# Four-part kernel on sample pipeline: modulation rows behind the first packing, w1 split ahead of head 0, its bias row in two parts, identity turns in TensorE's waits, last sample's stage by halves

## What is computed

```python
# block 0: adapter with an expert per sample, then a layer norm
hidden = gelu(x @ down_W.T + down_b); hidden = expert_W[dom] @ hidden + expert_b[dom] + domain_emb[dom]
x = layernorm(hidden @ up_W.T + up_b + x) * ln_gamma + ln_beta
# block 1: modulated attention with 16 heads of 16 columns, and a feed-forward of 1024
emb = silu(sin_emb(timestep)) @ W_ada + b_ada; scale, shift = split(emb)
x = ln(x) * (1 + scale) + shift
probs = softmax(mask(q @ k.T / 4 + attention_bias)); x = x + (probs @ v) @ Wo + bo
h = ln(x) * g2 + beta2;  x = x + gelu2(h @ W1 + b1) @ W2 + b2
# block 2: one of three MLPs per sample, added to x, then a layer norm
# block 3: f = x; f_new = relu(f + dt * (-grad(A f) + 0.5 * grad2(B f))), differences along rows and columns
```

## Time and profile before

| | |
|---|---|
| median of 3 runs | 862.34 us (861.21 to 862.44) |
| profiled execution | 859.46 us, its span 857.7 us |
| busy | PE 94%, DVE 86%, ACT 73%, POOL 19% of the span |
| mean granted TensorE clock | 0.979 |
| slowest chain by engine | PE 85%, DVE 7%, SPq 2%, DMA 2%, issue 2%, ACT 1% |

### The profile page before, as it was taken

How to read it: one execution, slowest core, us unless ns; L and a number is a source line. 1 busy time by engine, 2 the same in 40 slices (tenths; PEclk the granted TensorE clock), 3 DMA queues, 4 the chain that set the end, 5 groups by cost and what they waited for, 6 DMA issues and landing times.

```text
span 857.7 us, 18597 instructions
## 1 busy us (share of the span) xinstructions
PE 808.4 (94%) x5968; PEld 692.9 (81%) x5968; DVE 737.6 (86%) x2473; ACT 622.8 (73%) x1285; POOL 164.1 (19%) x160
## 2 busy tenths in 40 slices
PE   5697899999999999999999999999999999999992
PEld 2585688988888888988888888888888888887782
DVE  6577777998989898998989898998989898979687
ACT  3447687878788797878788797878788787677541
POOL 3110112030211222040211222030211222111020
PEclk9779999999999999999999999999999999999997
DMA  4968877685867867575767767585658767484100
GB/s 131 267 170 213 196 172 187 138 174 155 183 157 190 169 158 196 140 180 146 187 149 188 177 158 198 126 189 152 177 155 182 179 152 185 117 177 126 57 25 25
DMA packets 147610, 137.33 MB, mean 160 GB/s; under 512 B 19299, under 2 KB 144804, under 8 KB 147509
## 3 DMA queue, kind: packets, MB, share of 16 engines
q1 hardware_dynamic: 145652, 134.99, 64.7%
q10 hardware_dynamic: 1856, 1.07, 0.7%
HBM read 98.23 MB, written 4.23 MB: 119 GB/s over the span
## 4 chain that ended last, share of the span: by engine, by line
PE 85%; DVE 7%; SPq 2%; DMA 2%; issue 2%; ACT 1%; POOL 0%; ACTq 0%; POOLq 0%; DVEq 0%
PE back_bank L1406 13%; PE turn_bank L1362 12%; PE score_bank L1606 7%; PE context_bank L1416 7%; PE score_bank L1607 6%; PE attend_bank L1400 5%; PE back_bank L1400 5%; PE front_bank L1400 5%; PE front_bank L1455 3%; PE back_bank L1386 3%; PE back_bank L1377 3%; PE attend_bank L1386 3%; PE front_bank L1719 3%; PE attend_bank L1347 2%; PE front_bank L1446 2%
## 5 line engine op out<-in xcount | busy, mean ns | idle before, releaser
L581 ACT ACTIVATE sc<-sc,negmax 128x256 f32<-128x256 f32 x512 | 231.4, 504 | 15.4 <-DVE negmax L1236 14.0
L1236 DVE CUSTOM_DVE_ANT_0 sc<-score_bank,side 128x256 f32<-128x256 f32 x512 | 195.3, 419 | 36.7 <-PE score_bank L1607 32.3
L575 ACT ACTIVATE pt<-turn_bank 128x512 f32<-128x512 f32 x176 | 106.1, 604 | 132.0 <-PE turn_bank L1362 111.0
L1362 PE MATMUL turn_bank<-ident,sc 128*128 128x128 f32 x1024 | 156.6, 276 | 1.8 <-ACT sc L581 1.7
L1362 PEld LDWEIGHTS turn_bank<-ident,sc 128*128 128x128 f32 x1024 | 123.3, 141 | 32.3 <-issue 14.1
L1606 PE MATMUL score_bank<-ks,qs 128*128 128x256 f32 x512 | 122.9, 322 | 5.8 <-DMA qs<-ql 5.4
L1406 PE MATMUL back_bank<-w,ffT 128*128 128x256 f32 x512 | 118.5, 379 | 0.4 <-DVE ffT L1145 0.4
L1406 PEld LDWEIGHTS back_bank<-w,ffT 128*128 128x128 f32 x512 | 96.7, 190 | 13.5 <-DVE ffT L1145 1.0
L497 POOL TENSOR_TENSOR rstd<-var,half_neg 128x2 f32<-128x2 f32 x64 | 49.9, 780 | 282.5 <-DVE var L998 281.0
L1607 PE MATMUL score_bank<-mask_neg,ident_r 128*128 128x512 f32 x256 | 102.4, 400 | 0.0
L1606 PEld LDWEIGHTS score_bank<-ks,qs 128*128 128x128 f32 x512 | 78.7, 193 | 13.8 <-issue 10.6
(11 more groups left out here) (272 smaller groups left out, 1966.3 us busy)
## 6 DMA issues: line engine op xcount, KB each, us to landing
side<-in_side SPq DMA_DIRECT2D x128, 512.0 KB, 5.4
qs<-qh SPq DMA_DIRECT2D x128, 64.0 KB, 4.2
qs<-ql SPq DMA_DIRECT2D x128, 64.0 KB, 4.4
ks<-kh SPq DMA_DIRECT2D x120, 64.0 KB, 4.0
ks<-kl SPq DMA_DIRECT2D x120, 64.0 KB, 4.4
wb<-in_wb SPq DMA_DIRECT2D x15, 512.0 KB, 7.2
xN<-in_x SPq DMA_DIRECT2D x16, 256.0 KB, 4.7
wc<-in_wc SPq DMA_DIRECT2D x16, 256.0 KB, 2.8
```

The costliest lines, as they stand in the source:

```text
L575: e.activation(pt[:, h % NP2, :, :], two(tbank[h % 2]), ACT.Copy).then_inc(copied[h % 4], 1)
L581: i = e.activation(sc[:, h % NS, q, :], sc[:, h % NS, q, :], ACT.Exp, bias=negmax[:, q, h:h + 1], scale=-1.0)
L1236: i = e.tensor_tensor_reduce(sc[:, s % NS, q, :], two(sbank[s % 2])[:, q, :], side[:, (H * X.i + s) % NSIDE, q, :], -1.0, 3.4e38, ALU.add, ...
L1362: i = e.transpose(tbank[h % 2][:, k * S + q * P:k * S + q * P + P], sc[:, h % NS, q, k * P:k * P + P], ident[:, :])
```

## The change

- SP: w1 is loaded right behind the column pack, and the mask and side pair 0 stand ahead of sample 1's x. All five grids are loaded ahead of the store of the modulation rows. `load_ada` of sample 1 moves from slot 5 to slot 8 of turn -1, behind the q packs. In every turn the mask load now stands ahead of the x load.
- w1: ACT's high part moves into turn -2, DVE's low part into slot 10 of turn -1. PE makes the first half of the bias row ahead of head 0 and the second half in slot 6 of turn 0; DVE adds it in slot 11, and the edge columns (`set_edges`) move from slot 11 to slot 12.
- POOL clears only half of `ks`, DVE the other half at its start, with the context bank; clearing `vp` moves into turn -1. ACT fetches the gelu table ahead of its wait in turn -2.
- PE: `keep_busy(n)`, n turns of the identity into a score bank, 57 in all in eight calls: seven in turns -2 and -1, one ahead of head 0.
- Last sample: second feed-forward and third product of block 2 by halves in two banks, DVE's x3, x4 and steps by halves; the row differences are taken by fp32 products of r2 and u without parts (`differ_in_full`), and the product with grid c is added by PE with the identity; the relu and the store are by halves.

```diff
@@ SP
+            load(ld_w1, (w1_raw, blocks(d["w1"])))
...
-                load(ld_w1, (w1_raw, blocks(d["w1"])))
...
-                    if s == 0 and G and t not in (-2, 0):
-                        load_x(G)
                     if s == 0 and F:
                         wait(e, ev["mask_ready"], F.p)
...
+                            load_side(F, 0)
+                    if s == 0 and G and t not in (-2, 0):
+                        load_x(G)
+                        if t == -1:
+                            for c in (1, 2):
                                 load_side(F, c)
...
-                    if t == -1 and s == 5:
-                        e.wait_ge(st_ada, 16)
-                        load_ada(G)
                     if t == -1 and s == 6:
...
                     if t == -1 and s == 8:
+                        e.wait_ge(st_ada, 16)
+                        load_ada(G)
                         load_x(phase(t, 3))
@@ POOL
-            e.memset(ks[:, :, :].bitcast(F32), 0.0).then_inc(pool_set, 1)
...
+            e.memset(ks[:, 0:HM, :].bitcast(F32), 0.0).then_inc(pool_set, 1)
+
+            def set_values():
+                e.wait_ge(dve_set, KL0_SET)
+                e.memset(vp[:, :, :, :, :], 0.0).then_inc(pool_set, 1)
@@ ACT
                     if is_step(t, s, -2, 15):
+                        bring_gelu()
                         e.wait_ge(pe_set, ADA_DONE)
...
+                        e.wait_ge(ld_cols, 7 * 16)
+                        e.wait_ge(ld_w1, 16)
+                        for k in range(KT):
+                            e.activation(w1[:, k, :], w1_raw[:, k, :], ACT.Copy, scale=g2c[:, k:k + 1]).then_inc(act_set, 1)
                         e.wait_ge(pe_set, ROWS_DONE)
@@ DVE
+            e.memset(cbank[:, :], 0.0).then_inc(dve_set, 1)
+            e.memset(ks[:, HM:H, :].bitcast(F32), 0.0)
...
+            def last_steps(x):
...
+                e.scalar_tensor_tensor(out=t_e[:, :, :], in0=t_e[:, :, :], scalar=step, in1=fN[:, :, :],
+                                       op0=ALU.mult, op1=ALU.add).then_inc(ev["e_ready"], 1)
+                e.wait_ge(ev["e_ready"], x.n)
+                for q in range(TT):
+                    e.wait_ge(ev["d_done"], x.n + q)
+                    e.scalar_tensor_tensor(out=t_e[:, q, :], in0=two(HALF_D[q])[:, q, :], scalar=step, in1=t_e[:, q, :],
+                                           op0=ALU.mult, op1=ALU.add).then_inc(ev["w2s_ready"], 1)
...
-                                          (-1, 11, set_output_bias), (0, 3, lambda: set_first_low(0)), (0, 4, set_first_bias),
-                                          (0, 5, lambda: set_first_low(1)), (0, 7, set_scaled_grids), (0, 8, set_more_grids),
-                                          (0, 9, set_sum_grids), (0, 10, set_conditional), (0, 11, set_edges), (1, 9, set_derivatives)):
+                                          (-1, 10, set_first_low), (-1, 11, set_output_bias), (0, 7, set_scaled_grids), (0, 8, set_more_grids),
+                                          (0, 9, set_sum_grids), (0, 10, set_conditional), (0, 11, set_first_bias), (0, 12, set_edges), (1, 9, set_derivatives)):
@@ PE
+            def keep_busy(n):
...
+                for _ in range(n):
+                    e.transpose(sbank[1][:, 0:P], ident[:, :], ident[:, :])
...
+            def differ_in_full(x):
...
+                for m, src, ready in ((d2T, t_r2, "r2_ready"), (d1T, t_u, "u_ready")):
                     e.wait_ge(ev[ready], x.n)
                     for q in range(TT):
                         for k in range(KT):
...
+                            e.matmul(two(HALF_D[q])[:, q, :], m[:, k, q * P:q * P + P].bitcast(F32), src[:, k, :],
+                                     start=(m is d2T and k == 0), stop=False)
+                e.wait_ge(ev["gc_ready"], x.n)
+                for q in range(TT):
+                    e.matmul(two(HALF_D[q])[:, q, 1:D - 1], ident[:, :], t_c[:, q, 1:D - 1], start=False, stop=True).then_inc(ev["d_done"], 1)
...
                     if is_step(t, s, 0, 0):
                         e.wait_ge(act_set, ROWS_SET)
...
                         e.wait_ge(ev["ql_ready"], 1)
+                        e.wait_ge(ev["xa_ready"], 2)
+                        e.wait_ge(ld_w1, 16)
+                        first_bias(0, FM // 2)
+                        keep_busy(8)
...
+                    if is_step(t, s, 0, 6):
+                        first_bias(FM // 2, FM).then_inc(pe_set, 1)
```

More of the change, by code:

```diff
@@ L413, in body @@
                         if t == -1:
-                            for c in range(3):
+                            load_side(F, 0)
[3 more added lines that the diff above has]
+                            for c in (1, 2):
                                 load_side(F, c)
@@ L746, in body @@
                         e.activation(vp[:, F.par, :, :, 0:DH], two(fbank).rearrange("p t (h c) -> p t h c", h=H), ACT.Copy).then_inc(ev["v_ready"], 1)
-                        if t == -1:
-                            e.wait_ge(ld_w1, 16)
-                            for k in range(KT):
-                                e.activation(w1[:, k, :], w1_raw[:, k, :], ACT.Copy, scale=g2c[:, k:k + 1]).then_inc(act_set, 1)
                     if s == 10 and G and t != -1:
@@ L1351, in no_more, with first_bias @@
                 pass
+            def first_bias(m0, m1):
+                for m in range(m0, m1):
+                    for k in range(KT):
+                        i = e.matmul(bbank[:, m:m + 1], w1_raw[:, k, m * P:m * P + P], beta2c[:, k:k + 1], start=(k == 0), stop=(k == KT - 1))
+                return i
+            def keep_busy(n):
+                for _ in range(n):
+                    e.transpose(sbank[1][:, 0:P], ident[:, :], ident[:, :])
             def flips(x, h):
@@ L1470, in condition @@
                     project_T(bbank, wb, 0, x3T, KT, KT, no_more).then_inc(ev["b_done"], 1)
-            def differ_when_ready(x):
-                for m, parts, ready in ((d2T, (r2_h, r2_l), "r2l_ready"), (d1T, (u_h, u_l), "ul_ready")):
+            def differ_in_full(x):
+                for m, src, ready in ((d2T, t_r2, "r2_ready"), (d1T, t_u, "u_ready")):
                     e.wait_ge(ev[ready], x.n)
@@ L1477, in differ_when_ready, with second_half_ff @@
                         for k in range(KT):
-                            for n, part in enumerate(parts):
-                                i = e.matmul(two(fbank)[:, q, :], m[:, k, q * P:q * P + P], part[:, k, :], start=(m is d2T and q == 0 and k == 0 and n == 0),
-                                             stop=(m is d1T and q == TT - 1 and k == KT - 1 and n == 1))
-                i.then_inc(ev["d_done"], 1)
+                            e.matmul(two(HALF_D[q])[:, q, :], m[:, k, q * P:q * P + P].bitcast(F32), src[:, k, :],
+                                     start=(m is d2T and k == 0), stop=False)
+                e.wait_ge(ev["gc_ready"], x.n)
+                for q in range(TT):
+                    e.matmul(two(HALF_D[q])[:, q, 1:D - 1], ident[:, :], t_c[:, q, 1:D - 1], start=False, stop=True).then_inc(ev["d_done"], 1)
+            def second_half_ff(x, order):
+                for q, k in order:
+                    i = e.matmul(two(HALF_BANKS[q])[:, q, :], ffT[:, k, q * P:q * P + P], w2[:, k, :], start=(k == 0), stop=(k == FM - 1))
+                    if k == FM - 1:
+                        i.then_inc(ev["w2_done"], 1)
             def last_turns():
@@ L1546, in last_turns @@
                 condition(T, kind, wb_last)
+                differ(U, 1)
                 e.wait_ge(ev["gb_ready"], T.n)
-                project(bbank, gbT, wc, ev["c_done"], no_more)
+                for q in range(TT):
+                    for k in range(KT):
+                        i = e.matmul(two(HALF_BANKS[q])[:, q, :], gbT[:, k, q * P:q * P + P], wc[:, k, :], start=(k == 0), stop=(k == KT - 1))
+                    i.then_inc(ev["c_done"], 1)
                 e.wait_ge(ev["w_ready"], U.n)
-                differ_when_ready(T)
+                e.wait_ge(ev["x4_ready"], T.n + 1)
+                differ_in_full(T)
             def body(t):
```

137 lines of the change are left out of this document (86 added, 51 removed).

## The result

The changed kernel takes **852.51 us** (median of 6 runs, 851.41 to 854.92) against 862.39 us of the kernel before (median of 6, 858.55 to 863.12): a ratio of 0.9897, 95% interval [0.9873, 0.9921]. Forecast were 854.3 us in 850.5 to 859.0, and "faster". In a second set of runs the same kernel took 851.64 us against 861.32, 0.9888 [0.9867, 0.9909]. So 9 to 10 us went, where 8.0 were forecast.

The account below looks back on a forecast made before the run. The prediction took PE, busy for 94% of the span, to bound the middle turns, so only the two ends could move. Start 5.5 and end 2.5 us made 862.34 - 8.0 = 854.3 us, range 850.5 to 859.0.

Parts of the forecast that it names:

- The end, 2.5 us: Last sample's stage by halves, with differences taken without parts: 2.5 us gained, bounds 1.5 and 3.3.
- (b): Last sample, from u to the last relu's end, 7.1 us before: gains 1.1 to 2.3 us, taken as 1.5.
- (a): Last sample's x3, third product and x4 by halves: DVE starts as soon as it is free, 1.0 us gained.
- The start, 5.5 us: All up to turn 1: 5.5 us gained, near the middle of the SP terms, bounds 2.3 and 7.8.
- The first packing, -2.3: Head 0 waits for the last q pack; q packs start 3.8 us earlier, so head 0 gains 2.3 us.
- The clock, -1.9: Ahead of head 0, identity turns keep PE's clock at 2.4 GHz; k packs and head 0 gain 1.9 us.
- Rival 1: Identity turns ahead of x1 don't hold the clock and delay x1 by about 1 us: 856.8 us, chance 0.30.
- The bias row, -6.8 between heads 0 and 2: Turn 0: half the row ahead of head 0, half in slot 6, so 6.8 us go between heads 0 and 2.
- What is late next: SP and side: Turn 0: SP's queue and side pair 4 limit the gain; head 8 comes 4.7 to 6.7 us earlier.
- Rival 2: Turn 1 ends on a transfer, so all but 1 us of the start's gain is lost: 858.8 us, chance 0.12.
- Rival 3: Mask ahead of x delays block 0 in each of 14 turns; at 0.8 us per turn 865.5 us, chance 0.03.
- rival 4: More gain at both ends, start at 7.8 and last sample at 3.3 us: 851.2 us, chance 0.10.

Follow-up runs that it names:

- experiment 6: The kernel before with only the modulation rows' load moved from slot 5 to slot 8, behind the q packs: 860.76 us, ratio 1.0005.
- experiment 5: The changed kernel without the identity turns and with the bias row whole between heads 0 and 2: 851.49 us, ratio 0.9895 to the kernel before.
- experiments 4: The changed kernel with the whole bias row between heads 0 and 2 again, eight identity turns kept: 851.94 us, ratio 0.9892 to the kernel before.
- experiments 1: The changed kernel with all 57 identity turns left out: 852.02 us, ratio 0.9905 to the kernel before.
- experiment 7: The changed kernel with x loaded ahead of the mask again from turn 1 on: 852.26 us, ratio 0.9902 to the kernel before.

## Why the prediction was right or wrong

The time was right within 1.8 us, the sign and the range too. Step by step:

- **The end, 2.5 us: right.** 2.4 us behind the cut, in three profiles against eleven. Of it (b), u to the last relu, gained 1.9 (7.1 to 5.2 and 5.3; forecast 1.5); DVE's own chain, put at 4.7, was the bound: DVE works from u to 849.69 with 0.2 us of idleness. In the kernel before, too, it worked from u to 854.42 with no gap above 0.1 us. So what shortened the stage is work taken off DVE (two low parts and one addition) and a relu by halves. The pace of PE's products, on which the prediction spent most of its sum, was not the bound in either kernel. (a) was put at 1.0; product to x4 gave 0.6.
- **The start, 5.5 us: too small.** With 2.4 of the 9 to 10 us in the end, some 7 are ahead of the cut. The one profile shows 2.5 there (122.96 to 120.47), the other 7.1; each is one draw. The term that was too small is SP's: it was to come to x of sample 2 3.0 to 5.0 us earlier, and came 5.4 us earlier (37.95 to 32.51), and to side pair 4 6.5 us (55.62 to 49.13).
- **The first packing, -2.3, with the k packs landing at 38.4: wrong in its reason.** That step gave the last k pack the 2.7 us of a q pack. It took 5.95 us (8.90 in turn 1 of the second profile), and the k packs, not the q packs, set head 0 at 37.43 and 38.20, in place of the 36.5 of the sum. Undoing the move leaves head 0 at 37.69 and costs about 5 us: its worth lies in the time at which SP reaches the side pairs, which the prediction counted as the continuation of the same 3.8 us. Alone in the kernel before it is worth nothing (experiment 6).
- **The clock, -1.9: the clock came out as forecast, but that the turns cause it is only in part shown, and nothing of it is resolved in the time.** The clock is 1.00 from 20 to 30 us in ten profiles of ten with the turns, and in one of four without (0.67, 0.83, 0.83; 1.00 in experiment 5). Head 0 is at 39.06 and 38.72 without them, against 37.30 to 38.60 in the six profiles that have them and the same program up to there. Rival 1, which had the clock fall in spite of the turns, did not come true in any profile. The Trainium skill, in *TensorE: Matmul & The Clock Gate*, section "Part 4: PE-mode transpose", would have the transposes not count for the full rate. Here 20 of them from 19.13 us on, with the four turns of `xN` between, were followed by a turn of x1 of 0.66 us, and without them by one of 1.11 (twice), of 0.91, but once also of 0.66. That speaks against the page where a level is to be held, by a few executions; whether transposes raise the clock no run here shows.
- **The bias row, -6.8 between heads 0 and 2: right there, nothing at the end.** The prediction had said that most of it can't be collected. None of it was resolved in the time. The side pairs hide only part of it, as heads 2 and 6 move by 4.4 to 6.7 us and head 8 still by 2.8 to 3.6 (experiments 4 and 5), and the end does not move.
- **"What is late next: SP and side": the step that carries the result, and right.** Head 8 was put 4.7 to 6.7 us earlier; it is 6.3 (65.11 to 58.81) and 6.7 (to 58.44). The k packs make a second chain of nearly the same length: in turn 0 the profile's chain of waits goes through a k pack in the first profile of the changed kernel (31.44, 5.95 us) and through a side pair in the second (49.21, 7.79 us).
- **From head 8 to turn 1 "the work is the same": not quite.** Turn 1's head 0 gained 4.3 us in the first profile, 5.7 in the second; but it now waits 2.0 us for a pack, and the clock may fall behind that wait. Rival 2 holds in part: what the edits on PE win in turn 0 is lost again there in the profiles of experiments 1 and 5. The second profile still keeps 7.1 us at the cut, so most of the start's gain is not given back.
- **Rival 3: out** (experiment 7). What lies behind the cut got shorter by the 2.4 us of the end and no longer, so the middle turns did not change.

Of the checks that the prediction named, no wait at `load_ada`, the clock from 20 to 30 us, turn 1's head 0 at 78 to 80.5 (80.51 and 79.06) and 3.5 to 6 us for the last stage came in. Head 0 at 36 to 38 did in one profile (37.43) and not in the other (38.20). The q packs came in earlier than 27.5 to 29 (26.04), and x4 moved by 0.6, not 1. DVE stood still ahead of head 8 for 1.25 us in the first profile and not in the second.

That the time is so near the forecast owes something to luck: the start was taken near the middle of a range from 2.3 to 7.8 us, its first packing rested on the wrong packs, and the gain of about 9.5 us lies halfway between its own 8.0 and rival 4's 11.1.

**Open:** which of the untried edits (w1's earlier load and copy, half of `ks` cleared on DVE, `set_edges` one slot later) holds the rest. Undone one at a time, the tried ones account for about 5 us (rows) and 2.4 us (end) of the 9 to 10; by experiment 6 the first is not a term of its own. Open too is why the undone bias row costs nothing at the end, and what makes the pack of turn 1 late.

## What to carry to other kernels

An in-order queue that feeds several deadlines is costed at its last customer: read what stands behind the moved wait, down to the load that some engine stops for, before pricing the nearest one. When loads are moved together, undo each alone *and* do one alone: 5 us one way and 0 the other mean that the gain belongs to the combination. And when executions scatter by 5 us, cut every profile at one instruction that all kernels have: the part behind the cut here repeats within 0.7 us of its mean over the kernels with the same last stage, and priced the end where the medians could not.

## What was not expected of the hardware

- A 64 KB pack took 2.7 us to land in one stretch and 5.95 to 8.90 us in others. The DMA share of the stretch doesn't order these times: 1.02 from 30 to 40 us with the 2.7, 0.81 with the 5.95, 1.12 with 8.51. A landing time from one stretch is no price for another.
- The granted clock fell behind the same waits of PE (1.30 and 1.23 us) in one execution (0.71 from 90 to 100 us) and stayed at 1.00 in the other of the same kernel. Its cost, about 3 us in turn 1, is a good part of the scatter of 3 to 4 us between executions.
- PE at 213 ns for each product of one column (6.82 us for 32) shows as a busy PE at clock 0.50, in the kernel before and again in experiments 4 and 5; the first half of the same products at the higher level takes 115 ns each (1.84 us for 16).
